# One transfer instead of two for each q and k row group of a window-attention block (swin, 32 x 56 x 56 x 64)

## The reference, cut to what matters

```python
y = _ln(x, norm1_w, norm1_b)
y = jnp.roll(y, (-SS[0], -SS[1]), axis=(1, 2))
...
attn = jnp.einsum('bhnd,bhmd->bhnm', q, k) * scale
...
attn = attn + bias[None]
...
attn = jax.nn.softmax(attn.reshape(B * nW, h, N, N), axis=-1)
out = jnp.einsum('bhnm,bhmd->bhnd', attn, v).transpose(0, 2, 1, 3).reshape(B * nW, N, C)
...
z = jax.nn.gelu(z @ fc1_w.T + fc1_b, approximate=False) @ fc2_w.T + fc2_b
return x + z
```

## Time and profile before

| | us |
|---|---|
| median of 3 runs | 2191.48 (2190.91 to 2192.81) |
| the profiled execution | 2191.34 |
| its span, first to last instruction | 2189.5 |
| PE busy | 2140.3 (98%) |
| DVE, POOL busy | 1780.1 and 1772.9 (81%) |
| ACT busy | 1545.3 (71%) |
| q/k transfers: issues, size | 2048 of 49.0 KB |
| granted TensorE clock, mean | 0.993 |

### The profile page before, as it was taken

One profiled execution on the slowest core, in us unless ns is written; L12 is line 12 of the kernel. 1 busy time (PEld: TensorE's weight loads), 2 busy tenths in 40 slices (PEclk: granted clock), 3 DMA queues, 4 the chain that ended last, 5 costly groups with the idle time before them and its releaser, 6 DMA issues.

```text
span 2189.5 us, 148006 instructions
## 1 busy us (share of the span) xinstructions
PE 2140.3 (98%) x62790; PEld 1667.7 (76%) x62790; DVE 1780.1 (81%) x3231; ACT 1545.3 (71%) x2435; POOL 1772.9 (81%) x1687
## 2 busy tenths in 40 slices
PE   6999999999999999999999999999999999999997
PEld 3777777777777777777777777777777777777775
DVE  5788888888888888888888888888888888888874
ACT  4577777677677777767777776776777777777774
POOL 5788888888888888888888888888888888888874
PEclk8999999999999999999999999999999999999999
DMA  4232233222323332232323223233223333322321
GB/s 111 65 78 78 75 75 76 77 77 76 79 74 76 76 76 77 75 79 76 77 76 76 77 75 77 78 75 79 75 77 77 76 77 76 77 76 76 77 70 32
DMA packets 178587, 165.86 MB, mean 76 GB/s; under 512 B 21144, under 2 KB 152458, under 8 KB 178074
## 3 DMA queue, kind: packets, MB, share of 16 engines
q1 hardware_dynamic: 178074, 157.60, 28.0%
HBM read 28.99 MB, written 25.77 MB: 25 GB/s over the span
## 4 chain that ended last, share of the span: by engine, by line
PE 88%; DVE 4%; issue 3%; ACT 2%; SPq 2%; DMA 1%; DVEq 0%; POOL 0%; ACTq 0%; POOLq 0%
PE O L758 14%; PE S L722 11%; PE ST L744 10%; PE M L766 9%; PE ST L738 9%; PE M L829 9%; PE M L851 8%; PE M L814 5%; PE M L798 5%; PE M L784 4%; PE M L859 2%; PE S L726 2%; SPq L274 1%; DVE nm L582 1%; ACT gl L445 1%
## 5 line engine op out<-in xcount | busy, mean ns | idle before, releaser
L326 POOL TENSOR_TENSOR nmd<-diag,nm 121x392 f16<-121x392 f16 x1024 | 900.3, 892 | 288.1 <-DVE nm L582 234.1
L582 DVE TENSOR_REDUCE nm<-S 121x8 f16<-121x392 f32 x1024 | 574.3, 561 | 225.7 <-PE S L722 138.3
L426 ACT ACTIVATE pT<-ST 113x392 f32<-113x392 f32 x1024 | 506.9, 496 | 229.7 <-PE ST L744 224.9
L758 PEld LDWEIGHTS O<-vx,pT 113*49 113x49 f32 x16384 | 548.6, 126 | 45.1 <-issue 6.1
L758 PE MATMUL O<-vx,pT 113*49 113x18 f32 x16384 | 522.2, 196 | 3.8 <-issue 1.9
L722 PE MATMUL S<-kp,qp 128*49 128x49 f16 x16384 | 390.7, 186 | 11.0 <-DVE nm L582 7.9
L738 PE MATMUL ST<-qp,kp 128*49 128x49 f16 x16384 | 387.0, 185 | 2.4 <-issue 2.3
L722 PEld LDWEIGHTS S<-kp,qp 128*49 128x49 f16 x16384 | 313.0, 103 | 93.1 <-issue 55.5
L744 PE MATMUL ST<-nmd,shiftw 121*49 121x392 f16 x2048 | 354.4, 342 | 0.2 <-POOL nmd L326 0.2
L738 PEld LDWEIGHTS ST<-qp,kp 128*49 128x49 f16 x16384 | 324.8, 103 | 10.2 <-issue 2.3
L407 ACT ACTIVATE hl<-M 128x784 f16<-128x784 f32 x128 | 105.5, 824 | 309.1 <-PE M L784 229.3
(11 more groups left out here) (90 smaller groups left out, 3369.2 us busy)
## 6 DMA issues: line engine op xcount, KB each, us to landing
qp<-hl SPq DMA_DIRECT2D x1024, 49.0 KB
kp<-hl SPq DMA_DIRECT2D x1024, 49.0 KB
xin<-in_x SPq DMA_DIRECT2D x256, 98.0 KB
out<-res SPq DMA_DIRECT2D x256, 98.0 KB
kp<-in_c_keys SPq DMA_DIRECT2D x4, 588.0 KB, 7.2
weights<-in_c_weights SPq DMA_DIRECT2D x1, 448.0 KB, 4.4
bias_t<-spread SPq DMA_DIRECT2D x2, 73.5 KB, 2.2
shiftw<-in_c_shift SPq DMA_DIRECT2D x1, 139.0 KB
```

The source lines that it names most:

```text
L326: nc.gpsimd.tensor_tensor(nmd[j % LAG][:], diag[:], nm[j % LAG][:].unsqueeze(2).broadcast_to([RM, 2 * 4, N]), ALU.mult).then_inc(s_nmd, 1)
L426: nc.scalar.activation(pT[j % LAG][:].rearrange("k w h q -> k (w h q)"), ST[0:R, j % 2, 0:HK], ACT.Exp).then_inc(s_e, 1)
L582: V.tensor_reduce(nm[j % LAG][:], S[0:RM, 0:HK].rearrange("q (h n) -> q h n", n=N), AX_X, ALU.max, negate=True).then_inc(s_nm, 1)
L758: mm = MM(O[W0 * w:W0 * w + N, (4 * p + hp) * VC:(4 * p + hp + 1) * VC], pT[j % LAG][:, w, hp, :], vx[r % RING][:, window + 2 * w, hp, :], ...
```

## The change

The two halves of `qp` and of `kp` become one tensor each, with 784 columns a head in place of 392. A transfer carries both halves of a row group, so a unit has eight transfers of 98 KB. There is one semaphore for each buffer; PE waits for it at j = 0 only. `span` gives the column of a group in the wide tensor. The constant rows of k come in one load for each buffer, from an array that is twice as wide. The counts on `s_q` stay: eight transfers of 16 for a unit, 64 a unit on average over the two buffers.

```diff
-        qp = [[sb(f"qp{n}{b}", [128, HEADS, T], F16) for b in range(2)] for n in range(2)]
-        kp = [[sb(f"kp{n}{b}", [128, HEADS, T], F16) for b in range(2)] for n in range(2)]
+        qp = [sb(f"qp{n}", [128, HEADS, UT], F16) for n in range(2)]
+        kp = [sb(f"kp{n}", [128, HEADS, UT], F16) for n in range(2)]
...
             def load_keys(n):
-                for b in range(2):
-                    sp.dma_start(kp[n][b][0:BIAS], c_keys).then_inc(c_keys_in[n][b], 16)
+                sp.dma_start(kp[n][0:BIAS], c_keys).then_inc(c_keys_in[n], 16)
...
-            def spread_parts(u, r, b):
-                if b == 0:
-                    made, read = held(u + 1), held(U * u - U)
-                    sp.wait_ge(s_lo, made)
-                    if later(u, 2):
-                        sp.wait_ge(s_sh, read)
-                q, k = qp[r % 2][b], kp[r % 2][b]
+            def spread_parts(u, r):
+                made, read = held(u + 1), held(U * u - U)
+                sp.wait_ge(s_lo, made)
+                if later(u, 2):
+                    sp.wait_ge(s_sh, read)
+                q, k = qp[r % 2], kp[r % 2]
                 for qk, dst, order in ((0, q, (0, 1, 0, 1)), (1, k, (0, 1, 1, 0))):
                     for n, s in enumerate(order):
-                        part = hl[C * qk:C * qk + C, s, b].rearrange("m a t -> m (a t)")
-                        sp.dma_start(dst[BIAS + D * n:BIAS + D * n + D], part).then_inc(s_q[r % 2][b], 16)
+                        part = hl[C * qk:C * qk + C, s].rearrange("m b a t -> m (b a t)")
+                        sp.dma_start(dst[BIAS + D * n:BIAS + D * n + D], part).then_inc(s_q[r % 2], 16)
...
                 if later(u):
-                    for b in range(2):
-                        act.wait_ge(s_q[(r + 1) % 2][b], 64 * u + 64 - 64 * ((r + 1) % 2))
+                    act.wait_ge(s_q[(r + 1) % 2], 64 * u + 64 - 64 * ((r + 1) % 2))
...
             def span(j):
-                return T // 2 * (j % 2) + 2 * N * ((j % 4) // 2)
+                return T * (j // 4) + T // 2 * (j % 2) + 2 * N * ((j % 4) // 2)
...
-                if j % 4 == 0:
-                    pe.wait_ge(s_q[r % 2][b], 128 * (u // 2) + 128)
-                    if not later(u, 2):
-                        pe.wait_ge(c_q[u % 2][b], 1)
-                        pe.wait_ge(c_keys_in[u % 2][b], 16)
-                q, key, v = qp[r % 2][b], kp[r % 2][b], variant(r, j)
+                if j == 0:
+                    pe.wait_ge(s_q[r % 2], 128 * (u // 2) + 128)
+                if j % 4 == 0 and not later(u, 2):
+                    pe.wait_ge(c_q[u % 2][b], 1)
+                    pe.wait_ge(c_keys_in[u % 2], 16)
+                q, key, v = qp[r % 2], kp[r % 2], variant(r, j)
```

More of the change, by code:

```diff
@@ L129, in swin_block @@
         c_const_in = sem("c_const_in")
-        c_keys_in = [[sem(f"c_keys_in{n}{b}") for b in range(2)] for n in range(2)]
+        c_keys_in = [sem(f"c_keys_in{n}") for n in range(2)]
         c_zero = sem("c_zero")
@@ L157, in swin_block @@
         s_lo = sem("s_lo")
-        s_q = [[sem(f"s_q{n}{b}") for b in range(2)] for n in range(2)]
+        s_q = [sem(f"s_q{n}") for n in range(2)]
         s_vp = sem("s_vp")
@@ L288, in body @@
                 if on_chip(a):
-                    spread_parts(a, m + 1, 0)
-                    spread_parts(a, m + 1, 1)
+                    spread_parts(a, m + 1)
                 if isinstance(i, int) and i == -1:
@@ L392, in place_bias @@
                 act.wait_ge(c_bias, 1)
-                nc.scalar.activation(qp[n][b][0:BIAS].rearrange("p h (w q) -> p h w q", q=N),
+                nc.scalar.activation(qp[n][0:BIAS, :, T * b:T * b + T].rearrange("p h (w q) -> p h w q", q=N),
                                      bias_rows[:].unsqueeze(2).broadcast_to([BIAS, HEADS, 8, N]), ACT.Copy).then_inc(c_q[n][b], 1)
@@ L540, in place_bias @@
                 dve.wait_ge(c_bias, 1)
-                V.tensor_copy(qp[n][b][0:BIAS].rearrange("p h (w q) -> p h w q", q=N),
+                V.tensor_copy(qp[n][0:BIAS, :, T * b:T * b + T].rearrange("p h (w q) -> p h w q", q=N),
                               bias_rows[:].unsqueeze(2).broadcast_to([BIAS, HEADS, 8, N])).then_inc(c_q[n][b], 1)
@@ L730, in scores_T @@
             def scores_T(u, r, j):
-                q, key = qp[r % 2][j // 4], kp[r % 2][j // 4]
+                q, key = qp[r % 2], kp[r % 2]
                 if later(u) or j >= 2:
@@ L916, in shape_constants @@
     co = np.stack(np.meshgrid(np.arange(WIN), np.arange(WIN), indexing="ij")).reshape(2, -1)
-    keys = np.zeros((BIAS, HEADS, 8, N), np.float16)
+    keys = np.zeros((BIAS, HEADS, 16, N), np.float16)
     lopart = np.zeros((128, 1), np.float32)
@@ L940, in shape_constants @@
     line = (np.arange(-(WIN - 1), WIN, dtype=np.float32) / np.float32(WIN - 1)).astype(np.float32)
-    return ident, keys.reshape(BIAS, HEADS, 8 * N), lopart, diag.reshape(RM, 8, N), shiftw, line
+    return ident, keys.reshape(BIAS, HEADS, UT), lopart, diag.reshape(RM, 8, N), shiftw, line
 def kernel(x, L0_conv_norm1_w, L0_conv_norm1_b, L0_conv_qkv_w, L0_conv_proj_w, L0_conv_proj_b, L0_conv_cpb_w1,
```

## The result

| | before | after |
|---|---|---|
| median of 6 runs each, us | 2192.57 (2190.91 to 2194.25) | 2622.41 (2587.97 to 2632.38) |
| the profiled execution | 2191.34 | 2632.38 |
| its span | 2189.5 | 2630.6 |
| PE busy | 2140.3 | 2280.6 |
| granted TensorE clock, mean | 0.993 | 0.927 |

The ratio is 1.190, with a 95% interval of 1.184 to 1.197: the change makes the kernel 19% slower, where 0.5% faster was forecast. The ratio goes by the four faster runs of after: its two slowest, the profiled one among them, lie over 1.5% above its fastest.

The account below looks back on a forecast made before the run. The chain was taken as 88% TensorE, with the q/k transfers costing only at start-up: -5.2 - 2.7 - 2.3 - 0.8 + 0.3 = -10.7, from 2191.34 to 2180.6 us. Its own range was 2176 to 2186; the wider range reached 2190.

Parts of the forecast that it names:

- Time on the DMA engines: Engine time of one doubled q/k transfer: 0.65 to 1.34 us, taken as 0.70, plus 0.3 us of landing.
- The 75 and 107 GB/s: DMA rates read before the change: 75 at a steady burst's end, 107 in the catch-up behind the constant rows.
- the 12.25 us: Steady unit before the change: time from a burst's start to the next unit's first score matmul, 1004.15 to 1016.40.
- The slower rival: Each unit's first score waits for the whole transfer, stalling from 1.23 us a transfer: about 2300 us, chance 0.11.
- wait at j = 4 goes: PE's wait for a second half at j = 4 disappears, its rows coming with the first half's; priced at nothing.
- The start-up terms: Unit 3's xin lands near 37.6, -5.2 us; L407 of unit 3 near 62, released by its projection, -2.7 us.
- The clock term: TensorE's clock stays up after the start-up stalls: -2.3 us behind the second stretch, -0.8 behind the first.
- Steady state: In the steady part, waits behind a late split of q and k are absorbed, so the change gains 0 there.
- faster still: Steady jitter, 8 us over the run, comes from crowded DMA engines and goes: 2173 us, chance 0.12.
- bursts of 5.2 us: Sign of being right: SP issues a unit's eight transfers in 5.2 us, for 10.5 before.
- four units at 66.1: Sign of being right: in the steady part, four units in a row still take 66.1 us.
- the sign named for being wrong: Bursts of over 9 us, or a score matmul that waits for a DMA in every unit.

Follow-up runs that it names:

- the probe: Computation left out, zeros written; SP alone sends q/k-shaped copies in bursts: eight of 98 KB took 16.6 us into one group of neighbours, 7.3 into every fourth partition.
- the late wait alone: Changed kernel's wide tensors and single constant-row load, but sixteen transfers of 49 KB, PE waiting for both halves at j = 0: 2333.02 us, 1.068 of the kernel before.
- the interleaved kernel: The changed kernel with each transfer writing every fourth partition in place of eight neighbours: 2175.05 us, 0.994 of the kernel before.
- a step of two: The changed kernel with each transfer's eight partitions two apart, within sixteen, in place of neighbouring: 2189.58 us, 1.000 of the kernel before.

## Why the prediction was wrong

**The step that failed is "Time on the DMA engines".** It bounded the doubled transfer by 0.65 to 1.34 us and took 0.70. In the kernel after, a transfer took (1016.06 - 1001.52 - 2) / 8 = 1.57 us, outside the range (2 us for landing, an estimate from the probe). What paced it was neither bytes nor packets but the eight neighbouring partitions that it writes: into every fourth partition, the same transfers gave 2175.05 us for 2622.41. The bounds were scaled by bytes and packets from the rates in the earlier trace rows, and those rows did not hold what I used them for:

- The `xin` load at 154 GB/s writes 49 neighbouring partitions, a q/k transfer eight. I called it the nearest row by packet size; in what decides, the partitions written, it was the farthest.
- The 75 and 107 GB/s are sums over several transfers in flight, to different row groups; the window of 75 also holds part of an `xin` load. In the probe, changing groups gave 14.6 us a burst of 98 KB transfers where one group gave 16.6, and with 49 KB 13.3 against 17.3. The rate of a mixture says little of one transfer, and the overlap was better with the smaller ones.
- A burst of sixteen takes 10.5 us to issue and 13.3 to complete, so before the change SP's queue nearly hid the slow writes. Halving the issue time could only uncover them.

**The rule that I argued away was right.** The Trainium skill's rule on ports ("SBUF — State Buffer", section "Door 1: The DMA port swizzle") gave, as an estimate, 1.85 us a transfer, and I set "the trace shows 75 and 107" against it. By that rule the 12.25 us would have been overrun by 8 x 1.85 + 2.4 - 12.25 = 4.95 us a unit, an estimate that is above the 3.4 us that a unit lost (19.98 for 16.59). The test that decides, the same transfer with its rows interleaved, was one index away; the trace before held no such row.

**The slower rival had the mechanism and not the size.** First scores waiting for the whole transfer, decided from 1.23 us a transfer: shown by the late wait alone (+148 us). The 430 us have two more parts that no rival had: TensorE's stops for its instructions (141 us, beside 163 of waits), and 140 us of lower clock, which follows waits and stops alike. I gave this side 0.11 because I let one row overrule a rule, and cut the range at 2190 on the strength of it.

**The "wait at j = 4 goes" was priced at nothing** and is right taken alone, but it was half of an exchange: what went at j = 4 came at j = 0, where the deadline is half a unit earlier. With sixteen issues that exchange costs 148 us, with quick writes still some 64 (2247.93 against 2183.76, the kernel before with interleaved rows).

**The start-up terms can be read in the interleaved kernel**, where the failed step is taken out. `xin`'s row sum starts at 39.71 (before 42.84, forecast 37.6): 3.1 us of the 5.2. L403 of unit 3 starts at 64.31, not 62, and is released by the projection, as forecast. The clock term came:

```profile
38.00:44.00 6.00, 3.08 (x58) 2.32 (x59) 2.92 (x5) 1.85 (x4) 2.61 (x3) 0.77 0.50 169
68.00:79.00 11.00, 9.39 (x343) 8.34 (x337) 8.00 (x16) 4.10 (x9) 8.55 (x9) 1.00 0.32 95
```

These windows of the interleaved kernel show 0.77 for 0.57 and 1.00 for 0.53. By the projection at 79.53 for 86.19 the start has gained 6.7 us where -10.7 was summed, so the terms were right in kind and together 4 us too large. After that, 22 times four units took 1998.73 - 543.06 = 1455.67 us for 1460.06: 4.4 less. Steady state was priced at 0; the jitter that the "faster still" rival named goes in part. Together that is 11 us; the two profiled spans differ by 10.6 (2189.5 and 2178.9). Nothing of it reached the changed kernel itself, whose own first score of unit 0 came at 40.57 us, for 32.28.

**Of what was to be seen**, bursts of 5.2 us were right; four units at 66.1 were not (79.9, four times 19.98); the score that waits for a DMA, in 84 of 128 units, is the sign named for being wrong.

## What to carry to other kernels

Before making transfers larger, look at which partitions one of them writes: eight neighbours cost 1.8 us for 98 KB, eight rows four apart no more than their issue. With the rows interleaved the merging gained 9 us; with neighbouring rows it lost 430. A rate in the trace belongs to the mixture in flight there; to price one transfer, find a row with the same partitions or measure it alone. Merging transfers merges their deadlines too, so ask which consumer needs the first half and when.

## What was not expected of the hardware

- SBUF copies that no operand waits for can stop TensorE: four slow ones a unit cost 59 us (2237.16 against 2178.30), the same bytes interleaved next to nothing.
- A stop of 5.63 us was followed by a granted clock of 0.50 for at least the 6 us from 698 to 704, at 5.76 us of 6 busy. The 120 waits of the late-wait kernel, 0.98 us in the mean, left a mean clock of 0.988; the 84 of the changed kernel, 1.77 us in the mean, had 160 us at 0.50 behind them.
- Each of the 48 "issue" stops ended 1.33 to 1.86 us after a 16 KB instruction packet had. The supply of TensorE's written-out program goes over the DMA engines that the copies use: 495 packets, 1.4% of 16 engines' time.
- Issuing a 64-row transfer takes SP 613 ns at 49 KB and at 98 KB alike:

```profile
L272 SPq DMA_DIRECT2D qp<-hl x512: 613/614/1944, 24.0 to 2570.3; - x171
```

**Open**: what all of the 13 us are that a step of two loses to a step of four without waiting for transfers, and how slow writes hold an instruction packet up. A PE program small enough to loop would test whether the stops go with the supply; it was not tried. The fastest version found is the change with rows four apart, 2175.05 us.
